# Scaling z of all blocks but the last on GpSimd behind ScalarE copies, with new due steps, in a recurrent sandwich layer

## The reference, cut to what matters

```python
# x: (2, 1024, 512); hidden 1024; inner 1536
x = x + layernorm(y);  where, on layernorm(x):
    u = x @ W_in.T + b_in
    s_t = tanh(u_t + s_{t-1} * gamma + beta)      # 1024 steps, one after the other
    y = s @ W_out.T + b_out
x = x + layernorm(z);  where, on layernorm(x):
    gate = silu((x @ fp8(gate_w)) * gate_scale);  up = (x @ fp8(up_w)) * up_scale
    z = ((gate * up) @ fp8(down_w)) * down_scale
```

## Time and profile before

| what | value |
| --- | --- |
| median of 3 runs | 560.37 us (556.61 to 561.68) |
| profiled execution: its own time, and its span from first to last instruction | 556.6 us, 556.6 us |
| share of the span busy: PE, PEld, DVE, ACT, POOL | 97%, 82%, 80%, 67%, 41% |
| chain that ended last, share by engine | PE 67%, DVE 4%, ACT 1%, POOL 1% |

### The profile page before, as it was taken

The page is one execution under the profiler, slowest core; times in us unless marked ns, Lnnn a source line. Parts: engine busy times, 40 slices in busy tenths (PEclk is TensorE's granted clock), DMA queues, the critical chain, the costliest instruction groups (busy, mean ns, idle before and its releaser), DMA issues.

```text
span 556.6 us, 11947 instructions
## 1 busy us (share of the span) xinstructions
PE 540.2 (97%) x2958; PEld 457.6 (82%) x2958; DVE 444.8 (80%) x2608; ACT 374.8 (67%) x2317; POOL 228.0 (41%) x372
## 2 busy tenths in 40 slices
PE   8998989999899999999999999999999999999995
PEld 5846769888688888898889888987888887899994
DVE  3699999978797998878987899778988898874414
ACT  3687687864578777877678667876787777762332
POOL 1222446475446541652338222562341321633532
PEclk9999989999999999999999999999999999999998
DMA  8789398991104200120003000300002000200011
GB/s 275 248 268 250 83 226 154 258 158 40 46 13 153 60 1 1 56 80 2 1 2 114 20 1 2 109 6 2 1 2 77 1 2 2 76 2 1 1 39 38
DMA packets 25334, 39.92 MB, mean 72 GB/s; under 512 B 3761, under 2 KB 8497, under 8 KB 25265
## 3 DMA queue, kind: packets, MB, share of 16 engines
q1 hardware_dynamic: 19904, 30.24, 16.7%
q0 software_dynamic: 4608, 8.39, 8.9%
q10 hardware_dynamic: 752, 0.54, 0.3%
HBM read 26.57 MB, written 4.20 MB: 55 GB/s over the span
## 4 chain that ended last, share of the span: by engine, by line
PE 67%; DVE 4%; ACT 1%; POOL 1%; issue 0%; POOLq 0%; DVEq 0%; ACTq 0%
PE gate_up L1131 25%; PE wide L1087 15%; PE wide L1161 13%; PE wide L1056 12%; DVE recur L1231 1%; PE wide L1107 1%; DVE recur_second L1231 1%; ACT pairs L1556 1%; DVE z L1377 0%; DVE stats_z L1245 0%; POOL z L1744 0%; DVE fused L1364 0%; ACT gated L1591 0%; DVE x_lo L1346 0%; POOL norms L1669 0%
## 5 line engine op out<-in xcount | busy, mean ns | idle before, releaser
L1556 ACT ACTIVATE pairs<-recur 128x8 f32<-128x8 f32 x768 | 137.3, 179 | 90.3 <-DVE recur L1231 90.2
L1231 DVE TENSOR_TENSOR_SCAN recur<-recur,pairs 128x16 f32<-128x16 f32 x768 | 151.0, 197 | 48.1 <-ACT pairs L1556 45.8
L1556 ACT ACTIVATE pairs<-recur_second 128x8 f32<-128x8 f32 x768 | 136.8, 178 | 0.0
L1231 DVE TENSOR_TENSOR_SCAN recur_second<-recur_second,pairs 128x16 f32<-128x16 f32 x768 | 133.2, 173 | 0.0
L1754 POOL TENSOR_TENSOR fused_lo<-fused,fused_hi 128x256 fp32r<-128x256 f32 x95 | 70.4, 743 | 127.9 <-ACT fused_hi L1609 126.0
L1087 PE MATMUL wide<-w_out_sb,pairs 128*128 128x512 f32 (+1 forms) x272 | 112.5, 563 | 0.2 <-ACT pairs L1565 0.2
L1056 PE MATMUL wide<-x_norm_t,w_in_sb 128*128 128x256 f32 x448 | 102.7, 382 | 3.7 <-ACT x_norm_t L1507 3.7
L1056 PEld LDWEIGHTS wide<-x_norm_t,w_in_sb 128*128 128x128 f32 x448 | 84.6, 191 | 16.3 <-ACT x_norm_t L1507 4.3
L1087 PEld LDWEIGHTS wide<-w_out_sb,pairs 128*128 128x128 f32 x272 | 75.5, 298 | 25.9 <-ACT pairs L1565 0.7
L1161 PE MATMUL wide<-down_q,fused_hi 128*128 128x512 f32 x192 | 81.7, 425 | 1.9 <-POOL fused_lo L1754 1.9
L1591 ACT ACTIVATE gated<-gate_up,gate_scale_cols 128x128 f32<-128x128 f32 (+1 forms) x169 | 63.4, 378 | 27.0 <-PE gate_up L1131 26.8
(11 more groups left out here) (135 smaller groups left out, 777.2 us busy)
## 6 DMA issues: line engine op xcount, KB each, us to landing
x_res<-x SPq DMA_DIRECT2D x16, 256.0 KB, 3.3
x_in<-x SPq DMA_DIRECT2D x14, 256.0 KB, 4.6
out<-z SPq DMA_DIRECT2D x14, 256.0 KB, 2.5
x_norm_t<-x_t SPq DMA_DIRECT2D x5, 512.0 KB, 4.9
raw_own<-rounders POOLq DMA_DIRECT2D x9, 256.0 KB, 5.2
w_in_sb<-w_in_t SPq DMA_DIRECT2D x4, 512.0 KB, 7.0
w_out_sb<-w_out_t SPq DMA_DIRECT2D x8, 256.0 KB, 5.4
raw_own<-down_w SPq DMA_DIRECT2D x8, 256.0 KB, 4.7
```

The costliest lines, as they stand in the source:

```text
L1231: eng.tensor_tensor_scan(preact_of[b].rearrange("p c k -> p (c k)"), factors_of[b].rearrange("p c k -> p (c k)"), pairs[:, t % RING, colum ...
L1556: ins = eng.activation(pairs[:, t % RING + 1, columns, 0], preact_of[b][:, :, 1], ACT.Tanh)
```

## The change

In all blocks but the last, ScalarE copies z out of PSUM (`copy_z`, two halves of 256 columns per tile), GpSimd multiplies the whole tile by the down scale in place in SBUF (`scale_z`, 128x512), and VectorE's statistics of z wait for that. The waits for z's PSUM banks (by the transposes of x1 and by the first `down` of the last two blocks) are now on ScalarE's copies. The last block keeps VectorE's multiplication from PSUM. In the timetable six lengths, `PACE` (1.05 to 1.09) and all due steps of TensorE are new.

```diff
-U_STEPS, Y_STEPS, TRANSPOSE_STEPS, GATE_UP_STEPS, DOWN_STEPS, FIRST_U_STEPS, ROUND_STEPS = 7.0, 14.0, 1.0, 3.9, 1.9, 7.4, 2.8
+U_STEPS, Y_STEPS, TRANSPOSE_STEPS, GATE_UP_STEPS, DOWN_STEPS, FIRST_U_STEPS, ROUND_STEPS = 7.14, 14.4, 0.91, 3.876, 1.934, 7.4, 2.77
...
-CHUNKS_FROM = [132.6999999999995, 268.39999999999856, 380.8000000000002, 538.3000000000013, 671.1000000000012, 894.2000000000016, 988.8000000000003, 1038.600000000004]
+CHUNKS_FROM = [-542.4, -404.9, -345.7, 291.2, 837.6, 425.4, 685.7, 572.8]
...
-PACE = 1.05
+PACE = 1.09
...
+        if n < LAST:
+            for h in range(row_parts("z", n, b, LAST)):
+                side("scalar", ("z_copy", n, b, h), [(after, BEHIND_TENSOR)] + stored, k if k_copy is None else k_copy)
+            side("gpsimd", ("z_scale", n, b), [(v, 0.2) for v in rows("z", "z_copy", n, b)], k, RESIDUAL_STEPS)
         for h in range(row_parts("z", n, b, LAST)):
-            side("vector", ("z_copy", n, b, h), [(after, BEHIND_TENSOR)] + stored, k if k_copy is None else k_copy)
-            side("vector", ("z_half", n, b, h), [(("z_copy", n, b, h), 0.0)], k)
+            if n == LAST:
+                side("vector", ("z_copy", n, b, h), [(after, BEHIND_TENSOR)] + stored, k if k_copy is None else k_copy)
+            side("vector", ("z_half", n, b, h), [(("z_copy", n, b, h), 0.0)] if n == LAST else [(("z_scale", n, b), BEHIND_POOL)], k)
...
-                            eng.wait_ge(s_z_scaled, rows_through("z", n - 1, b))
+                            eng.wait_ge(s_z_copied, rows_through("z", n - 1, b))
...
+            def copy_z(b):
+                for n in range(LAST):
+                    for h in row_pieces("z", n, b):
+                        yield at["z_copy", n, b, h]
+                        if h == 0:
+                            eng.wait_ge(s_z_psum, n * batch + b + 1)
+                            if n > 0:
+                                eng.wait_ge(s_stored, 16 * batch * n)
+                        eng.copy(z[:, b, row_slice("z", n, b, h)], wide[2 + b][:, row_slice("z", n, b, h)]
+                                 ).then_inc(s_z_copied, 1)
...
+            def scale_z(b):
+                for n in range(LAST):
+                    yield at["z_scale", n, b]
+                    if n == 0:
+                        eng.wait_ge(s_rows_in, 32)
+                    eng.wait_ge(s_z_copied, rows_through("z", n, b))
+                    eng.tensor_tensor(z[:, b, :], z[:, b, :], down_scale_rows[:, :], ALU.mult).then_inc(s_z_scaled, 1)
```

More of the change, by code:

```diff
@@ L146 @@
 DOWN_RANK, NEGATE_RANK, ISSUE_RANK, PEAK_RANK, FIRST_X1_RANK, FIRST_CHUNKS_RANK = 20.0, 0.0, -2.0, 150.0, -4.0, -3.0
-CHUNKS_FROM = [132.6999999999995, 268.39999999999856, 380.8000000000002, 538.3000000000013, 671.1000000000012, 894.2000000000016, 988.8000000000003, 1038.600000000004]
[L151 to L154, removed]
+CHUNKS_FROM = [-542.4, -404.9, -345.7, 291.2, 837.6, 425.4, 685.7, 572.8]
+CHUNKS_PER_BLOCK = [102.5, 48.5, 29.0, 17.5, 25.0, 92.5, 43.5, 31.5]
+INPUTS_FROM = [-1473.6, -66.4, 429.7, 1277.2, 732.8, 626.9, 1401.1, 1772.7]
+ROWS_FROM = [-533.8, -629.9, 21.1, 568.3, -166.0, 164.2, 918.5, 258.4, 1615.2, 492.7, 1050.9, 1620.9, 1287.0, 919.2, 2359.7, 856.2]
+ROWS_TURNED = [-211.6, -7.4, -53.7, -37.6, 612.2, 667.5, -102.4, 72.0, 1051.3, 171.5, -14.8, 402.8, 1606.5, 316.3, 905.8, 1064.8]
 TENSOR_MARGIN = 1.0
@@ L742, in recurrent_sandwich_kernel @@
         s_z_psum = sem("s_z_psum")
+        s_z_copied = sem("s_z_copied")
         s_z_scaled = sem("s_z_scaled")
+        s_last_z_scaled = sem("s_last_z_scaled")
         s_z_norm = sem("s_z_norm")
@@ L1158, in down_products @@
                                 else:
-                                    eng.wait_ge(s_z_scaled, rows_through("z", p - 1, b))
+                                    eng.wait_ge(s_z_copied, rows_through("z", p - 1, b))
                             for part in (fused_hi, fused_lo):
@@ L1366, in fuse, with scale_last_z @@
                                                      op0=ALU.mult, op1=ALU.mult).then_inc(s_fused, 1)
[L1368 to L1378, removed]
+            def scale_last_z(b):
+                for h in row_pieces("z", LAST, b):
+                    cols_of = row_slice("z", LAST, b, h)
+                    yield at["z_copy", LAST, b, h]
+                    if h == 0:
+                        eng.wait_ge(s_z_psum, LAST * batch + b + 1)
+                        eng.wait_ge(s_stored, 16 * batch * LAST)
+                    eng.tensor_tensor(z[:, b, cols_of], wide[2 + b][:, cols_of], down_scale_rows[:, cols_of],
+                                      ALU.mult).then_inc(s_last_z_scaled, 1)
             def measure_z(b):
@@ L1383, in measure_z @@
                         yield at["z_half", n, b, h]
-                        eng.wait_ge(s_z_scaled, rows_through("z", n, b, h))
+                        if n < LAST:
+                            eng.wait_ge(s_z_scaled, n * batch + b + 1)
+                        else:
+                            eng.wait_ge(s_last_z_scaled, rows_through("z", n, b, h) - rows_through("z", LAST - 1, batch - 1))
                         part_stats("z", z, n, b, h)
@@ L1650, in store_last @@
                     eng.dma_start(out_blocks[LAST][1][:, g, :], z[1:P:batch, g, :]).then_inc(s_last_stored, 16)
-            weave(center_last_z(), store_last(), first_loads(), warm_up(), sign_identity(), negate_constants(), copy_x(), copy_first_u(), copy_u(), recurrence(), high_x1(), gates(),
+            weave(center_last_z(), store_last(), first_loads(), warm_up(), sign_identity(), negate_constants(), copy_x(), copy_first_u(), copy_u(), recurrence(), high_x1(), gates(), copy_z(0), copy_z(1),
                   high_parts(), take_weights())
```

5 lines of the change are left out of this document (3 added, 2 removed).

## The result

The change takes 575.87 us (median of 4 runs, 575.41 to 577.32) against 559.39 us (4 runs, 556.61 to 561.68) for the kernel before: 1.030 times as long, with a 95% interval of 1.025 to 1.035. It is slower, as forecast (571.5), and by more than forecast. Medians and ratios are of the runs; times inside a kernel are of its profiled execution, whose span is 573.6 us for the change.

What follows compares the result with a forecast made beforehand. TensorE's pace was taken to bound the kernel from 144 to 550 us, with the scans a near second limit. 556.6 - 6.0 + 17.4 = 568.0 us, plus 3.8 for the median of runs, said as 571.5; range 562 to 578.

Steps and rivals of the forecast that it cites:

- start, to step 256: First 144 us: head and TensorE's work about the same, so zero; bounds a 3.7 us gain, a 2 us loss.
- two-chain stretch: The 767 scan steps that took 351.5 us before; forecast to get 6.0 us shorter.
- tail: Behind the last scan: more chunks of block 6 left for TensorE, 17.4 us longer, between 16.1 (held by a semaphore) and 18.8.
- What bounds the kernel: Between 144 and 550 us the kernel runs at TensorE's pace; the scans, at 0.442 us a step, are a near second limit.
- What the scans get back: Two-chain stretch: scans no longer held by TensorE as a rule; 6.0 us of 12.5 excess regained, bounds 1.0 and 12.5.
- GpSimd multiplies: z products on GpSimd, 14 x 1.29 us, none on the path while z's statistics stand several steps behind.
- Rival B: Around the last scan GpSimd's queue delays low part 1, TensorE idles 3 to 6 us; 573 us, 577 on median's scale; chance 0.13.
- The forecast's own sign: Profile after: last scan at 487 to 492 us, TensorE's last matmul some 70 us behind it.
- ScalarE copies: z's 24 half copies in the two-chain stretch lengthen steps by 0.5 us at most in total; 0.2 us taken.
- The scale of the runs: Profiled execution taken as 3.8 us under the median of runs, so 568.0 became 571.8, said as 571.5.
- Rival A: Over the 1024 steps, moved TensorE work lets scans run earlier: 556.5 us, 560.3 on the median's scale, no change; chance 0.14.
- Rival C: Two-chain stretch: VectorE bounds, removing 9.7 us from it shortens the scans; 546.9 us, 550.7 on the median's scale; chance 0.03.

Runs made afterwards that it cites:

- e3: The change, with each GpSimd z product also waiting for the x1 sums the plan puts ahead of it: 570.44 us, 1.0208 times the kernel before.
- e5: The kernel before, with the products of the low part left out of every `down` (45 us less TensorE work): 548.26 us, 0.9824 times the kernel before.
- e2: The kernel before, z still on VectorE, with the change's job lengths, `PACE` 1.09 and due steps: 572.48 us, 1.0237 times the kernel before.
- e9: The change with `PACE` 1.05, z products also waiting for x1 sums and normalizations planned ahead of them: 1.0018 times the kernel before.
- e1: The change's move of z, with lengths, `PACE` and due steps of before (one 20 steps earlier): 562.94 us, 1.0066 times the kernel before.
- e6: The change, with the products of the low part left out of every `down`: 568.34 us, 1.0184 times the kernel before.
- e1b: As e1, with z products also waiting for x1 sums and normalizations planned ahead of them: 559.69 us, 1.0009 times the kernel before.
- e8: The change with `PACE` 1.00, z products also waiting for x1 sums and normalizations planned ahead of them: 1.0216 times the kernel before.
- e11: The change with `PACE` 1.07, z products also waiting for x1 sums and normalizations planned ahead of them: 1.0114 times the kernel before.

## Why the prediction was right, and where it was off

By its own steps, in the spans of the profiled executions (the column of e3 is the change without held sums):

| term | forecast | change | e3 |
| --- | --- | --- | --- |
| start, to step 256 | 0 | -1.1 | -0.4 |
| two-chain stretch (351.5) | -6.0 | +0.4 | -5.2 |
| tail (61.0) | +17.4 | +17.7 | +17.7 |
| span (556.6) | 568.0 | 573.6 | 568.7 |

- **What bounds the kernel.** Right, and smaller than it sounds: e5 shows that TensorE, idle for 0.9 of 351.5 us, held the scans by 5.1 us only. A saturated engine and one that sets the time are not the same.
- **The tail.** Right to 0.3 us, and part of that is luck. The count put 68.8 us of work from `gate_up` of chunk 4 on, and it takes 69.0. Between the bounds of 16.1 and 18.8 the forecast chose 17.4 for no more than the middle; what happened is the case of the upper one, both pieces behind the last scan, which measured 17.7. The semaphore that was to hold the tail was not waited for, since TensorE came to that `gate_up` late. e2 shows that the tail belongs to the timetable, and e9 that within the timetable it is mostly `PACE`: 66.8 us at 1.05.
- **What the scans get back.** The 6.0 us were right but for 0.8 us: the stretch of e3 is 5.2 us shorter, and e5 gets about as much by another way. How they divide over the single items of the forecast is not shown, but for the waits of y. In the change VectorE no longer waits for y in this stretch, where it did for 2.7 us. They are not seen in the change because the next term takes them back.
- **GpSimd multiplies: "nothing of it is on the path".** This is the step that failed. The duration was right (1.27 us against 1.29), and z's statistics hardly wait for it. But while a product runs, a sum or a normalization on VectorE is held, and seven sums took 5.8 us out of the scans. Rival B knew that an operation that stands still in VectorE's queue holds every scan behind it, but had one that waits for a semaphore; here none waits for one. The forecast's own sign, the last scan at 487 to 492, failed (494.9). A last scan at 495 was read in advance as "the excess was not TensorE's lateness". About 5 us of it were (e5), and they did come back, but a new cost of the same size took their place. The trace of before could not show it, since of its 90 sums and normalizations in that stretch none starts inside a GpSimd operation wider than one column, and their medians are 327 and 322 ns. Nothing binds the product to its place in the timetable, which has it behind the last sum; the semaphore that it waits for is that of ScalarE's copies, and it starts early. The Trainium skill, "SBUF — State Buffer", section SBUF: two separate sides, would have named the term: VectorE and GpSimd share a pair of ports as an exclusive lock for a whole instruction, against VectorE operations that use two ports or take two inputs from SBUF. This case's traces agree: sums of 1.12 to 1.24 us beside products of 1.27 us, and 0.32 to 0.46 us without (e3). That a normalization is held as well (1.10 to 1.13 us in e1) fits that rule only by its half on two ports, and no row here shows how many ports it uses.
- **ScalarE copies.** 367 ns each; a step with one has a median of 0.442 us by the starts of the scans. The 0.2 us were nothing.
- **The scale of the runs.** 3.8 us were added because the span of 556.6 was taken for the run of 556.61 us. Each later profiled execution is 1.8 or 1.9 us longer than its span (575.41 against 573.6), so the profile before more likely belongs to the run of 558.41 us that came with the result. That hid a part of the miss: the forecast is 5.6 us short in spans, and 4.4 us short in medians.
- **Rival A (work conserved)** fell with e6, where 31.5 us of idle TensorE time do not speed up one scan. **Rival C (VectorE the bound)** fell with e1b: 24 operations of 406 ns less on VectorE, and the time is the same. **Rival B** had the sign and roughly the size, 573 in spans, but its place was wrong: TensorE has no gap behind the last scan in the change. It appears in e5, where TensorE has less to do.
- **A sum in rival A.** Half of its 16.2 us left out makes 560.3 + 8.1 = 568.4 us, and not 563. The outcome does not touch it.

Open: with the old due steps e1b has 28 steps over 0.53 us and before 22. They add up to 8.6 us over 0.442 each against 6.0, which covers the 2.2 us by which e1b's stretch is longer, and no run took them apart. e9 is level with before but for 0.2% (the interval is 1.0001 to 1.0036), and no run looked for due steps with which the z halves would pay.

## What to carry to other kernels

When work moves to GpSimd, ask not only whether its result is in time, but which VectorE operations run while it does: a side operation of 0.33 us with a serial chain behind it lasts as long as what is left of GpSimd's own, and an order that keeps them apart on paper needs a semaphore to keep them apart on the chip. In a kernel with a serial chain and a saturated engine beside it, a stretch in the plan (`PACE`) trades waits inside the chain against work left over behind it: too low and side operations stand ahead of their input (e8), too high and the tail grows by about 3 us a chunk (66.8, 72.6 and 78.7 us with six, eight and ten chunks in e9, e11 and e3). A length in a plan is worth a run of its own: one number, 1.09 for 1.05, was most of this loss. Take an engine's share of the bound from an experiment that removes its work, not from its busy time.

## What the runs showed of the hardware

A VectorE sum of 128 columns with two SBUF inputs that starts inside a wide GpSimd operation ends 0.14 to 0.15 us after that operation, whether the latter has two inputs (1.27 us) or one (0.62 us); a sum of 256 columns ends 0.28 us after it (the first of the change), and a normalization of 128 columns, with one tensor, 0.08 us (e1, and beside the one-input operation of 0.76 us in e2). GpSimd's operations on one column (the roots, up to 0.81 us) hold nothing that can be seen: normalizations that start in them with 0.25 to 0.43 us left take 322, 328 and, for 256 columns, 393 ns in e3, against medians of 322 and 389. Nor are VectorE's other operations in the change held when they start inside a wide operation of GpSimd: the scans take 0.17 to 0.20 us, the statistics of 128 columns (one tensor in SBUF) 265 to 276 ns in 20 places against 268 elsewhere, and `fuse` (one of its two tensors in PSUM) 323 to 353 ns in 24 places against 326.

Neither busy share of TensorE alone tells what it has left. Before, weight loads are busy 86% of a stretch in which matmuls leave 0.9 us idle and the chunks start right behind one another; so the other 14% were not to be had, against the rule of the Trainium skill that the prediction weighed ("Perfetto Trace Analysis", section Identifying the Most-Contended Engine). But the matmuls' busy time, which that rule warns of, misleads as well. In e3, 104 matmuls fewer stand in the stretch than before, some 17 us by the starts in the earlier trace rows: 76 of `gate_up`, 20 of `down` and 8 of y. The weight loads' busy time is 16.9 us less (284.1 against 301.0), the matmuls' only 8.1 (342.5 against 350.6). For the difference between these two kernels the weight loads are the better measure.
